# Four graph layers in one kernel: layer 1 aggregates before it multiplies, and the end of layer 3 is ordered anew

## The chip, the cores and the metric

The kernel runs on one core of a Trainium2 chip. The metric is the device time of one execution in microseconds; each time given for a kernel is the median of several runs. Four engines compute: TensorE (PE, matrix products and transposes), VectorE (DVE), ScalarE (ACT) and GpSimd (POOL). SyncE (SP) issues most transfers.

## The reference

The graph has 1024 nodes of 512 features and 16384 edges from `src` to `dst`. Four layers follow each other, each inside `x = layernorm(x + layer(x))`:

```
L0: h = x @ W0 + b0;  adj = row-normalised symmetric 0/1 adjacency with self loops
    relu(dw0*h + dw1*adj@h + dw2*adj@adj@h + dw3*adj@adj@adj@h)
L1: agg = segment_sum(x[src], dst);  agg @ W1.T + b1
L2: x @ wc + segment_sum((x @ wn)[dst], src) / counts + bias
L3: per head h of 8:  Wx = x @ Ws[h] + Wb[h]   (64 columns)
    s = leaky_relu(Wx[dst].a1 + Wx[src].a2 + ab);  alpha = softmax of s over the edges of a dst
    out_h = segment_sum(alpha * Wx[src], dst)
```

In layer 1 the sum over edges is linear. With C the matrix of edge counts, C (x W1^T) = (C x) W1^T, so the product by the weights may stand on either side of the gather.

## The kernel before, in words

**Tiles.** Nodes lie in 8 tiles of 128. `xcur` holds x, `cst` the counts C (source in partitions, target in columns) in f16, `cts` its transpose, `adj` the adjacency. The eight PSUM banks `ps[:, 0..7]` hold 512 f32 columns each. For precision an f32 value is held as two f16 numbers, high and low: a product by weights is three matmuls for each of four blocks of 128 features (hi*hi, hi*lo, lo*hi; `three`, L723), so 12 per tile of 128 nodes and 512 columns; a product by C is two (C is exact).

**Order.** Each engine executes its own queue in the order written, and semaphores join them. No planner is involved: the order is what the text says. Loops over tiles (`Fori`) run two tiles per turn.

**The end of layer 0.** The third hop (`step`, L911) makes one tile of 16 matmuls after another into bank t. `total0` (L1414) takes each from its bank with two VectorE operations and raises `y_ready`. `moments` and `scales` (L1353, L1345) on VectorE and `norm` (L525) on ScalarE make the norm; ScalarE writes the high part into `cur[:, 1, 0]` and the f32 value into `xcur`; GpSimd (L409, L412) then makes the low part (`x_lo`) and adds the next bias (`xb_ready`).

**Layer 1.** TensorE transposes each tile of x (`transposes`, L902: 8 matmuls of 128x128 per tile), ScalarE copies it to `xTs` (`xT_evict`, L536), TensorE multiplies by W1 (`products1`), ScalarE and VectorE take the result z from PSUM as high and low part (`z_hi`, `z_lo`), and `gather` (L953) multiplies by C: 16 matmuls of 512 columns per tile. The transposes of tiles 0 and 1 stand ahead of the third hop's last tile; those for layer 2 ahead of the gather's last tile. `total1` (L1444) adds the result to x, and the norm follows as before. Layer 2 has two products per tile (wc and wn) and another gather.

**Layer 3's beginning.** Per tile TensorE makes x @ W3 and the score columns, ScalarE two exponentials (`exps`, L546), VectorE `wx_evict` (L1466) and `y_whole` (L1474, an operation of 128x1024 f32 from two SBUF inputs), ScalarE the high part of y (`y_upper`), and VectorE the low part (`y_lower`, L1479, two SBUF inputs too). For tiles 5 and 6 GpSimd makes the low part (L417). `exps` of tile t waits for the low part of tile t-2, whose buffer `yf` it reuses. Behind the last y, VectorE computes a bound of the scores (`lim`, L1505 to L1509), TensorE transposes it (L1057), and VectorE turns it into the flag (L1512, L1513) on which all engines branch (`mode`). TensorE meanwhile multiplies y by C (`dense_part`, L1026), four early units tile by tile, the other twelve after the branch. The scores u go through memory (`u_rows`, SP, L331 and L335) and come back as rows for the masks.

**Heads.** For each of 8 heads VectorE makes 8 masks (L1525 or, from a row that ScalarE prepared at L645, L1529), TensorE 8 tiles of 16 matmuls (`head_tile`, L1086). `combine_open` (two VectorE operations from PSUM, L1543 and L1546) and `combine_close` (three, L1552 to L1557) turn a head's sums into output; GpSimd adds it to `xcur` (L424). The tables `OPEN_AT` and `CLOSE_AT` say after which mask each stands.

**Tail.** Heads 6 and 7 are done together in three groups of tiles (`LAST_BANKS`: 0-2, 3-5, 6-7). ScalarE scales their sums (`scaled_sum`, L624), `last_sum` (L1565) does the rest on VectorE, with the norm's statistics over the last 128 columns; `stats` (L1559) takes those of the other columns, `last_moments`, `last_scales` and the norms (`NORM_ACT` on ScalarE, L668, `NORM_DVE` on VectorE, L1597) end a group, and SP sends each tile out, in order of tiles (L341).

Of the kernel before, what the change touches and what calls it, by code (L numbers as in the profile page):

```python
# [26 lines left out]
P = 128  # L27
N = 1024
D = 512
# [27 lines left out]
ASCALE = 1.0 / 32  # L57
# [22 lines left out]
OPEN_AT = {31: 0, 38: 1, 43: 2, 49: 3, 55: 4, 63: 5}  # L80
# [3 lines left out]
STAT_COLS = (0, 5 * DH, PAIR * DH, D)  # L84
NORM_ACT, NORM_DVE = (0, 1, 3, 4, 6), (2, 5, 7)
# [10 lines left out]
def build(nc, x, xT, src, dst, W0, b0, dw, W1T, b1, wc, wn, b2, W3, W3T, b3, b3T, aw, ab, out):  # L96
    with ExitStack() as ctx:
# [248 lines left out]
        def _(pool):  # L346
# [92 lines left out]
        def _(act):  # L439
# [85 lines left out]
            def norm(layer, t, i):  # L525
# [6 lines left out]
                if layer < 3:  # L532
                    act.activation(cur[:, 1, 0, t, :], xcur[:, t, :], ACT.Identity, bias=b, scale=r).then_inc(S["x_hi"], 1)  # L533
                act.activation(xcur[:, t, :], xcur[:, t, :], ACT.Identity, bias=b, scale=r).then_inc(S["x_ready"], 1)  # L534

            def xT_evict(layer, t, i):  # L536
                act.wait_ge(S["xT_done"], t + (layer * NT + 1))
# [3 lines left out]
            def z_hi(layer, t, i):  # L541

                act.wait_ge(S["z_done"], t + (layer * NT + 1))
                copy(cur[:, 0, 0, t, :], ps[:, 4 + i, :], 1 / WSCALE).then_inc(S["z_hi"], 1)

            def exps(t, i):  # L546
                act.wait_ge(S["uvc_done"], t + 1)
                if isinstance(t, int) and t == NT - 1:
                    act.wait_ge(S["y_lo_pool"], 1)
                else:  # L550
                    act.wait_ge(S["y_lo"], t + 1)
# [10 lines left out]
            for layer in range(3):  # L562
# [5 lines left out]
                if layer == 0:  # L568
                    act.wait_ge(S["w_lo"], 4)
                    act.wait_ge(S["cnt_row"], 1)  # L570
# [3 lines left out]
                if layer < 2:  # L574
                    xT_evict(layer, 2, 0)
                    z_hi(layer, 0, 0)
# [20 lines left out]
                else:  # L597
                    with act.Fori(0, NT // 2 - 2) as r:
                        for i in (1, 0):
                            t = r * 2 + (2 - i)  # L600
                            z_hi(layer, t, i)
                            xT_evict(layer, t + 2, i)
                    xT_evict(layer, NT - 1, 1)
                    z_hi(layer, NT - 3, 1)
                    z_hi(layer, NT - 2, 0)
                    z_hi(layer, NT - 1, 1)
# [10 lines left out]
            with act.If(flag(act, 2)):  # L617
                act.activation(std[:, 0:1], epsc[:], ACT.Sqrt).then_inc(S["warm"], 1)

                def sum_of(h, t):  # L620
                    return ps[:, 2 + 2 * (t // 3) + h - PAIR, t % 3 * YW:t % 3 * YW + DH + 1]
# [42 lines left out]
                def last_norms(b):  # L664
                    act.wait_ge(S["scale8"], b + 1)
                    for t in range(*LAST_BANKS[b]):
                        if t in NORM_ACT:
                            act.activation(xcur[:, t, :], xcur[:, t, :], ACT.Identity, bias=nmr[:, t:t + 1],  # L668
                                           scale=rstd[:, t:t + 1]).then_inc(S["out_act"], 1)

                act.wait_ge(S["warm"], 3)
                for b in range(2):
# [4 lines left out]
                last_norms(0)  # L677
                scaled_sums(PAIR + 1, 2)
                deviations(1)
                last_norms(1)  # L680
                deviations(2)
                last_norms(2)
            with act.Else():
                act.wait_ge(S["y_lo"], NT)
                act.wait_ge(S["y_lo_pool"], 2)
# [34 lines left out]
        def _(pe):  # L720
# [206 lines left out]
            transposes(0, 0, 0)  # L927
            transposes(0, 1, 1)
            step(NT - 1, False)

            def per_tile(layer, products, before_last=None):
# [9 lines left out]
                pe.wait_ge(S["xT_in2"], layer * NT + NT - 2)  # L941
# [6 lines left out]
            def product(layer, name, bank, done, free, n, t):  # L948
                pe.wait_ge(S["xT_in2"], t + (layer * NT + 1))
# [3 lines left out]
            def gather(layer, c16, left, done):  # L953

                pe.wait_ge(S["xT_in2"], (layer + 1) * NT)
                pe.wait_ge(S["y_ready"], (layer + 1) * NT)

                def tile(t, parts, first=False):
                    for c in parts:
                        for j in range(NT):  # L960
                            if first:
                                pe.wait_ge(S["z_lo"], layer * NT + j + 3)
                            for v in range(2):
                                ins = mm(ps[:, t, :], c[:, j, bass.ds(t * P, P)], cur[:, 0, v, j, :],  # L964
                                         start=c is c16 and j == 0 and v == 0,
                                         stop=c is parts[-1] and j == NT - 1 and v == 1)
                    ins.then_inc(S[done], 1)

                def tiles(parts):
# [4 lines left out]
                    transposes(layer + 1, 0, 0)  # L974
                    transposes(layer + 1, 1, 1)
                    tile(NT - 1, parts)

                pe.wait_ge(S["big_in"], 1)
                with pe.If(flag(pe, 1)):
                    if layer == 0:  # L980
                        pe.wait_ge(S["left_in"], NT)
                        with pe.Fori(0, NT) as t:
                            pe.wait_ge(S["left_t"], t + 1)
                            for j in range(NT):
                                ins = pe.transpose(bank16(7)[:, j * P:(j + 1) * P], c_left[:, j, bass.ds(t * P, P)], id16[:])
                            ins.then_inc(S["left_done"], 1)
                        pe.wait_ge(S["left_t"], NT + 1)
                    tiles((c16, left))
                with pe.Else():
                    tiles((c16,))  # L990
# [776 lines left out]
```

## Time and profile before

| | us |
|---|---|
| median of 3 runs (415.71 to 415.84) | 415.73 |
| the profiled execution's own time | 415.07 |
| its span, first to last instruction | 413.3 |
| TensorE busy | 381.1 (92%) |
| VectorE busy | 281.0 (68%) |
| ScalarE busy | 249.1 (60%) |
| GpSimd busy | 97.4 (24%) |
| mean granted TensorE clock, share of full | 0.992 |

A line of the timeline gives the start within the span, the length, engine, line of the kernel, what is written and read, and in brackets the idle time before it and what ended that. Matmul lengths overlap their neighbours, so TensorE's pace is read from the distance of two starts. Operations of one kind in a row are merged; their count stands behind the x.

### The profile page before, as it was taken

How to read it: one execution, taken by the hardware profiler on the slowest of the kernel's cores; microseconds unless marked ns; L12 is line 12 of the kernel's file. 1: busy time of each engine (PE TensorE's matmuls, PEld its weight loads, DVE VectorE, ACT ScalarE, POOL GpSimd, SP SyncE). 2: the span in 40 equal slices, each digit the busy share in tenths (PEclk: the TensorE clock that was granted, in tenths of full speed). 3: DMA queues.
4: the chain of work that ended last, by engine and by line, in shares of the span. 5: the costliest groups of instructions: out<-in, count | busy, mean ns of one | idle time of the engine just before them, and what ended most of it. 6: DMA issues, size and time to landing. Idle time of an engine off the chain costs nothing. (4 is left out here: it accounts for less than half of the span.)

```text
span 413.3 us, 8534 instructions
## 1 busy us (share of the span) xinstructions
PE 381.1 (92%) x2908; PEld 227.0 (55%) x2908; DVE 281.0 (68%) x604; ACT 249.1 (60%) x404; POOL 97.4 (24%) x87
## 2 busy tenths in 40 slices
PE   1799888999999999899999999999897999999990
PEld 1344436544444454444445444445555889999990
DVE  7678999729994774225533222554698588999995
ACT  9789777485712356613545221257674899999433
POOL 4520000049900275302644000133104000021110
PEclk9999999999999999999999999999999999999996
DMA  5940005005000000000000000000000313130005
GB/s 193 389 145 2 1 1 205 2 0 205 0 0 2 0 0 2 0 2 1 2 0 2 0 0 2 0 2 0 2 0 8 100 51 103 54 100 7 2 3 207
DMA packets 10040, 18.53 MB, mean 45 GB/s; under 512 B 2128, under 2 KB 2320, under 8 KB 10000
## 3 DMA queue, kind: packets, MB, share of 16 engines
q1 hardware_dynamic: 9136, 14.86, 10.4%
q10 hardware_dynamic: 864, 3.15, 2.4%
q8 instruction: 24, 0.39, 0.4%
q14 instruction: 16, 0.13, 0.1%
HBM read 15.87 MB, written 2.13 MB: 44 GB/s over the span
## 5 line engine op out<-in xcount | busy, mean ns | idle before, releaser
L732 PE MATMUL ps<-big,xTs 128*128 128x512 f16 x384 | 86.2, 379 | 2.9 <-ACT xTs L441 2.9
L732 PEld LDWEIGHTS ps<-big,xTs 128*128 128x128 f16 (+1 forms) x384 | 36.6, 98 | 44.6 <-issue 3.1
L645 ACT ACTIVATE big<-big,uvt 128x1024 bf16<-128x1024 f32 x55 | 58.9, 1149 | 0.0
L409 POOL TENSOR_TENSOR big<-xcur,big x24 | 27.7, 1156 | 128.4 <-ACT xcur L534 128.4
L533 ACT ACTIVATE big<-xcur,nmr,rstd (+1 forms) x24 | 19.5, 813 | 37.8 <-DVE nmr L1351 37.8
L441 ACT ACTIVATE big<-ps 128x512 f16<-128x512 f32 (+2 forms) x25 | 14.5, 579 | 42.1 <-PE ps L732 32.7
L765 PE MATMUL ps<-big,xTs 128*128 128x512 f32 x64 | 34.7, 638 | 0.0
L1361 DVE SCALAR_TENSOR_TENSOR big<-ps,big 128x512 f32 (+1 forms) x16 | 11.0, 690 | 31.0 <-ACT big L441 31.0
L383 POOL TENSOR_TENSOR big<-xTs,big 128x2048 f16<-128x2048 f32 x4 | 16.3, 4097 | 58.8 <-ACT big L441 58.8
L1029 PE MATMUL ps<-big,cst 128*128 128x260 f16 x256 | 29.9, 275 | 0.0
L786 PE MATMUL ps<-adj,cts 128*128 128x80 f16 (+31 forms) x128 | 21.1, 268 | 8.9 <-DVE c L1245 4.7
L1245 DVE TENSOR_TENSOR c<-c,ps 128x80 f32 (+31 forms) x64 | 23.1, 362 | 9.1 <-PE ps L786 5.9
L786 PEld LDWEIGHTS ps<-adj,cts 128*128 128x128 f16 x128 | 11.2, 107 | 31.3 <-issue 15.9
L916 PE MATMUL ps<-big,adj 128*128 128x512 f16 x128 | 28.1, 379 | 0.0
L441 ACT ACTIVATE xTs<-ps 128x1024 f16<-128x1024 f16 (+1 forms) x24 | 23.9, 1017 | 6.9 <-PE ps L908 6.9
L964 PE MATMUL ps<-big,cts 128*128 128x512 f16 x128 | 28.0, 379 | 0.0
L964 PE MATMUL ps<-big,cst 128*128 128x512 f16 x128 | 28.0, 379 | 0.0
L898 PE MATMUL ps<-big,adj 128*128 128x512 f16 x128 | 27.8, 379 | 0.0
L1029 PEld LDWEIGHTS ps<-big,cst 128*128 128x128 f16 x256 | 24.2, 96 | 4.7
L464 ACT ACTIVATE cts<-iota_lo,early 128x128 f16<-128x128 f16 x80 | 25.4, 391 | 0.4
L424 POOL TENSOR_TENSOR xcur<-xcur,c 128x512 f32<-128x512 f32 x6 | 7.1, 1183 | 69.4 <-DVE c L1557 69.4
L1226 DVE TENSOR_TENSOR adj<-adj,early 128x160 f16<-128x160 f16 (+31 forms) x64 | 22.3, 388 | 0.1
(205 smaller groups left out, 689.3 us busy)
## 6 DMA issues: line engine op xcount, KB each, us to landing
big<-u_rows ACTq DMA_DIRECT2D x6, 512.0 KB, 3.6
xTs<-in_xT SPq DMA_DIRECT2D x2, 1024.0 KB, 9.2
xcur<-in_x SPq DMA_DIRECT2D x1, 2048.0 KB, 17.6
out<-xcur SPq DMA_DIRECT2D x8, 256.0 KB, 2.2
big<-in_W SPq DMA_DIRECT2D x1, 1024.0 KB, 5.9
cts<-in_W3T SPq DMA_DIRECT2D x1, 1024.0 KB, 13.1
xTs<-in_W1T SPq DMA_DIRECT2D x1, 1024.0 KB, 5.3
xTs<-in_wc SPq DMA_DIRECT2D x1, 1024.0 KB, 8.2
```

Source lines behind the costliest of these rows:

```text
L409: pool.tensor_tensor(cur[:, 1, 1, t, :], xcur[:, t, :], cur[:, 1, 0, t, :], ALU.subtract).then_inc(S["x_lo"], 1)
L441: return act.activation(o, i, ACT.Copy, scale=scale, **kw)
L464: act.activation(square[:, i % 2, c, :], iota_lo[:], ACT.Square, bias=chunks(nslo[:], mine[i])[:, c:c + 1]).then_inc(S["lo_square"], 1)
L645: act.activation(above[:, a % AHEAD, :], uf[:, h % 2], ACT.Relu, scale=BIG, bias=vb[:, j, h:h + 1]).then_inc(S["above_in"], 1)
L732: return mm(bank, lhs(k)[a], rhs(k)[b], start=start and k == 0 and n == 0, stop=stop and k == KT - 1 and n == 2)
L765: ins = mm(bank, xT32[:, k, t * P:(t + 1) * P], w0raw[:, k, :], start=k == 0, stop=k == KT - 1)
L786: ins = mm(ps[:, WINDOW_BANKS[w % 4], 0:n], left, hot_key[:, r, w % 2 * NC * n:(w % 2 + 1) * NC * n].rearrange("p (k c) -> p k c", c=NC)[: ...
L898: ins = mm(ps[:, t, :], adj[:, j, t * P:(t + 1) * P], cur[:, 1, v, j, :], start=n == 0 and v == 0, stop=n == NT - 1 and v == 1)
L916: ins = mm(ps[:, t, :], adj[:, j, bass.ds(t * P, P)], cur[:, 0, v, j, :], start=n == 0 and v == 0, stop=n == NT - 1 and v == 1)
L964: ins = mm(ps[:, t, :], c[:, j, bass.ds(t * P, P)], cur[:, 0, v, j, :], start=c is c16 and j == 0 and v == 0, stop=c is parts[-1] and j == ...
L1029: ins = mm(ps[:, DENSE_BANK[i], 0:4 * (DH + 1)], cst[:, j, t * P:(t + 1) * P], yh[:, j, v, 4 * half:4 * half + 4, DH + 1:YW], start=j == 0 ...
L1245: tt(cells, cells, ps[:, WINDOW_BANKS[w % 4], 0:NT * m].rearrange("p (a w) -> p a w", w=m), ALU.add).then_inc(S["win_free"], 1)
```

## The change

Layer 1 first multiplies x by the counts, with x as the stationary and C as the moving operand, which gives the aggregate already transposed in eight banks (four blocks of features times two halves of the nodes). ScalarE and VectorE take them into `xTs` as high and low part (`agg_hi`, `agg_lo`), and the product by W1 writes its tiles into banks 0 to 7. The transposes of x and the evictions of z in layer 1 are gone. In layer 3's beginning, the low parts of y of tiles 5 and 6 are made by VectorE. In the tail, head 5's sums are scaled by ScalarE, `stats(0)` covers 256 columns and stands ahead of head 5's close, `stats(1)` covers 128 and stands behind `last_sum(0)`, and ScalarE makes all norms but that of tile 7. Some semaphore increments that nobody waits for are dropped.

```diff
-ASCALE = 1.0 / 32
+ASCALE = 1.0 / 8
-OPEN_AT = {31: 0, 38: 1, 43: 2, 49: 3, 55: 4, 63: 5}
+OPEN_AT = {31: 0, 38: 1, 43: 2, 49: 3, 55: 4}
-STAT_COLS = (0, 5 * DH, PAIR * DH, D)
-NORM_ACT, NORM_DVE = (0, 1, 3, 4, 6), (2, 5, 7)
+STAT_COLS = (0, 4 * DH, PAIR * DH, D)
+NORM_ACT, NORM_DVE = (0, 1, 2, 3, 4, 5, 6), (7,)
@@ GpSimd
-            for t in (NT - 3, NT - 2):
-                pool.wait_ge(S["y_hi"], t + 1)
-                pool.tensor_tensor(yh[:, t, 1], yf[:, t % 2].rearrange("p h e d -> p h (e d)"), yh[:, t, 0],
-                                   ALU.subtract).then_inc(S["y_lo_pool"], 1)
@@ ScalarE
+            def agg_hi(a):
+                act.wait_ge(S["agg_done"], a + 1)
+                half, k = a // KT, a % KT
+                copy(xTs[:, 0, k, half * HALF:(half + 1) * HALF], ps[:, a, :], ASCALE).then_inc(S["agg_hi"], 1)
-            for layer in range(3):
+            with act.Fori(0, NT // 2) as r:
+                for i in range(2):
+                    norm(0, r * 2 + i, i)
+            act.wait_ge(S["w_lo"], 4)
+            for a in range(NT):
+                agg_hi(a)
+            for layer in range(1, 3):
...
+                h = PAIR - 1
+                act.wait_ge(S["head_done"], h + 1)
+                act.wait_ge(S["x_added"], h - 1)
+                for t in range(NT):
+                    scaled_sum(h, t)
                 for b in range(2):
                     scaled_sums(PAIR, b)
                     scaled_sums(PAIR + 1, b)
                 deviations(0)
                 scaled_sums(PAIR, 2)
-                last_norms(0)
+                last_norm(0)
+                last_norm(1)
                 scaled_sums(PAIR + 1, 2)
+                last_norm(2)
                 deviations(1)
-                last_norms(1)
+                last_norm(3)
+                last_norm(4)
                 deviations(2)
-                last_norms(2)
+                last_norm(5)
+                last_norm(6)
@@ TensorE
             pe.wait_ge(S["big_in"], 1)
-            transposes(0, 0, 0)
-            transposes(0, 1, 1)
             step(NT - 1, False)
+            def aggregate(parts):
+                for half in range(2):
+                    for j in range(NT):
+                        pe.wait_ge(S["x_lo"], j + 1)
+                        for k in range(KT):
+                            for c in parts:
+                                for v in range(2):
+                                    ins = mm(ps[:, half * KT + k, :], cur[:, 1, v, j, k * P:(k + 1) * P],
+                                             c[:, j, half * HALF:(half + 1) * HALF],
+                                             start=c is cst and j == 0 and v == 0,
+                                             stop=c is parts[-1] and j == NT - 1 and v == 1)
+                            if j == NT - 1:
+                                ins.then_inc(S["agg_done"], 1)
+            pe.wait_ge(S["y_ready"], KT)
+            with pe.If(flag(pe, 1)):
...
+            with pe.Else():
+                pe.wait_ge(S["y_ready"], NT)
+                aggregate((cst,))
+            def product1(t):
+                three(ps[:, t, :], cols(xTs, t), weight("W1")).then_inc(S["linear1_done"], 1)
+            pe.wait_ge(S["agg_lo"], KT)
+            for t in range(KT):
+                product1(t)
+            pe.wait_ge(S["agg_lo"], NT)
+            for t in range(KT, NT - 1):
+                product1(t)
+            transposes(1, 0, 0)
+            transposes(1, 1, 1)
+            product1(NT - 1)
...
-            def products1(t, i):
-                product(0, "W1", 4 + i, "z_done", "z_lo", t + 1, t)
-            per_tile(0, products1)
-            products1(NT - 1, 1)
-            gather(0, cst, c_left, "gather1_done")
@@ VectorE
-            norm_loop(0, total0, products_in1)
-            products_in1(1, 1)
-            with dve.Fori(1, NT // 2) as r:
-                for i in range(2):
-                    products_in1(r * 2 + i, i)
+            norm_loop(0, total0)
...
+            def agg_lo(a):
+                half, k = a // KT, a % KT
+                nodes = slice(half * HALF, (half + 1) * HALF)
+                dve.wait_ge(S["agg_hi"], a + 1)
+                stt(xTs[:, 1, k, nodes], ps[:, a, :], ASCALE, xTs[:, 0, k, nodes], ALU.mult, ALU.subtract).then_inc(S["agg_lo"], 1)
+            for a in range(NT):
+                agg_lo(a)
             def total1(t):
-                dve.wait_ge(S["gather1_done"], t + 1)
+                dve.wait_ge(S["linear1_done"], t + 1)
                 dve.wait_ge(S["xb_ready"], t + 1)
-                tt(xcur[:, t, :], ps[:, t, :], xcur[:, t, :], ALU.add).then_inc(S["y_ready"], 1)
+                stt(xcur[:, t, :], ps[:, t, :], 1 / (WSCALE * ASCALE), xcur[:, t, :], ALU.mult, ALU.add).then_inc(S["y_ready"], 1)
...
             y_whole(NT - 2, 0)
+            y_lower(NT - 3, 1)
             wx_evict(NT - 1, 1)
...
             stt(lim[:, 3:4], lim[:, 1:2], VMAX * BIG, lim[:, 3:4], ALU.is_le, ALU.mult).then_inc(S["lim_in"], 1)
+            y_lower(NT - 2, 0)
             y_lower(NT - 1, 1)
...
+                def combine_scaled(h):
+                    c = comb[:, h % 2].rearrange("p (a b) d -> p a b d", a=3)
+                    dve.wait_ge(S["head_done"], h + 1)
+                    dve.wait_ge(S["scaled"], NT)
+                    tt(c, c, sums(h)[:, :, :, DH + 1:YW], ALU.subtract).then_inc(S["comb_ready"], 2)
...
-                combine_close(H - 3)
                 stats(0)
+                combine_scaled(PAIR - 1)
+                combine_close(PAIR - 1)
+                last_sum(0)
                 stats(1)
-                last_sum(0)
                 last_moments(0)
                 last_sum(1)
                 last_moments(1)
-                dve.wait_ge(S["scale8"], 1)
-                last_norm(2)
                 last_sum(2)
                 last_moments(2)
-                dve.wait_ge(S["scale8"], 2)
-                last_norm(5)
                 last_scales(2)
                 dve.wait_ge(S["scale8"], 3)
                 last_norm(7)
```

`scaled_sum` and `sums` take head 5's banks in the new version; `c_left` and `ct_left` serve only the branch for counts above 2048, which isn't taken here.

## Rows read from the trace of the kernel before

**Rows 1.** The page's head: span; busy time and share of each engine, with instructions.

```profile
span 413.3 us, 8534 instructions
PE 381.1 (92%) x2908; PEld 227.0 (55%) x2908; DVE 281.0 (68%) x604; ACT 249.1 (60%) x404; POOL 97.4 (24%) x87
```

**Rows 2.** Busy by window: length, then each engine's busy us, clock, DMA share, GB/s.

```profile
156.79:181.75 24.96, 23.73 (x146) 12.07 (x145) 7.82 (x15) 14.36 (x21) 7.12 (x7) 1.00 0.00 1
181.75:210.27 28.52, 28.52 (x146) 13.42 (x145) 13.93 (x34) 12.17 (x21) 11.92 (x10) 1.00 0.00 1
```

**Rows 3.** TensorE's timeline: start, length, line, operation, count, idle time before and its releaser.

```profile
152.45 1.06 PE L908 MATMUL ps<-id,big 128*128 128x128 f16 x16
...
153.34 3.62 PE L916 MATMUL ps<-big,adj 128*128 128x512 f16 x16
156.79 2.75 PE L732 MATMUL ps<-big,xTs 128*128 128x512 f16 x12
159.38 0.61 PE L908 MATMUL ps<-id,big 128*128 128x128 f16 x8
...
167.45 2.76 PE L732 MATMUL ps<-big,xTs 128*128 128x512 f16 x12 [1.23 <-ACT xTs L441]
```

**Rows 4.** Timeline of VectorE, then GpSimd, around the third hop's tiles 3 and 7.

```profile
142.62 0.75 DVE L1416 SCALAR_TENSOR_TENSOR acc<-ps,winv,acc  x1 [0.44 <-PE ps L916]
...
157.78 0.69 DVE L1419 SCALAR_TENSOR_TENSOR xcur<-acc,xcur 128x512 f32<-128x512 f32 x1
...
151.10 1.16 POOL L409 TENSOR_TENSOR big<-xcur,big  x1 [0.96 <-ACT xcur L534]
```

**Rows 5.** Timeline of VectorE, then ScalarE, in layer 1's norms before.

```profile
188.99 0.69 DVE L1447 TENSOR_TENSOR xcur<-ps,xcur  x1 [1.84 <-PE ps L964]
...
191.07 0.21 DVE L1351 TENSOR_SCALAR nmr<-mv,rstd 128x1 f32 x1
...
206.57 1.94 ACT L441 ACTIVATE xTs<-ps 128x1024 f16<-128x1024 f16 x2
```

**Rows 6.** Timeline, layer 3's beginning: VectorE, GpSimd, TensorE, ScalarE.

```profile
308.53 1.22 DVE L1476 TENSOR_TENSOR acc<-cts,acc 128x1024 f32<-128x1024 f32 x1
309.66 1.24 DVE L1481 TENSOR_TENSOR big<-acc,big 128x1040 f16<-128x1040 f32 x1
...
311.61 2.55 DVE L1476 TENSOR_TENSOR acc<-cts,acc 128x1024 f32<-128x1024 f32 x1
...
315.77 2.81 DVE L1476 TENSOR_TENSOR acc<-cts,acc 128x1024 f32<-128x1024 f32 x1
...
321.18 0.14 DVE L1513 CAST flags<-lim 1x1 int32<-1x1 f32 x1
...
310.93 2.15 POOL L417 TENSOR_TENSOR big<-acc,big 128x1040 f16<-128x1040 f32 x1 [20.53 <-ACT big L441]
315.34 2.16 POOL L417 TENSOR_TENSOR big<-acc,big 128x1040 f16<-128x1040 f32 x1 [2.26 <-ACT big L441]
...
316.00 0.27 PE L1054 MATMUL ps<-id,uvt 128*64 128x128 f32 x1 [1.54 <-DVE uvt L1472]
...
319.22 0.27 PE L1057 MATMUL ps<-id,lim 128*1 128x128 f32 x1 [1.11 <-DVE lim L1509]
...
322.18 1.28 ACT L618 ACT_TABLE_LOAD   x1 [2.35 <-DVE flags L1513]
```

**Rows 7.** Timeline of the tail: VectorE, TensorE, ScalarE.

```profile
383.11 4.89 DVE L1529 TENSOR_TENSOR cts<-big,cst 128x1024 f16<-128x1024 bf16 x8
...
392.68 4.25 DVE L1563 BATCH_NORM_STATS2 early<-xcur 128x6 f32<-128x320 f32 x16
...
400.59 0.56 DVE L1572 TENSOR_TENSOR c<-c,ps 128x390 f32<-128x390 f32 x1
...
394.12 2.88 PE L1091 MATMUL ps<-big,xTs 128*128 128x130 f16 x48
...
408.99 0.81 ACT L668 ACTIVATE xcur<-xcur,nmr,rstd 128x512 f32<-128x512 f32 x1 [0.43 <-DVE nmr L1594]
```

More of the change, by code:

```diff
@@ L547, in exps @@
                 act.wait_ge(S["uvc_done"], t + 1)
[L548 to L551, printed above, removed]
+                act.wait_ge(S["y_lo"], t + 1)
                 for e, f in enumerate((1.0, SLOPE)):
@@ L575, in _ @@
                     xT_evict(layer, 2, 0)
-                    z_hi(layer, 0, 0)
+                    z_hi(0, 0)
                 norm(layer, NT - 2, 0)
@@ L620, in sum_of @@
                 def sum_of(h, t):
+                    if h < PAIR:
+                        return ps[:, 2 + 3 * (h % 2) + t // 3, t % 3 * YW:t % 3 * YW + DH + 1]
                     return ps[:, 2 + 2 * (t // 3) + h - PAIR, t % 3 * YW:t % 3 * YW + DH + 1]
@@ L940, in per_tile @@
                 transposes(layer, NT - 2, 0)
-                pe.wait_ge(S["xT_in2"], layer * NT + NT - 2)
+                pe.wait_ge(S["xT_in2"], (layer - 1) * NT + NT - 2)
                 transposes(layer, NT - 1, 1)
@@ L948, in product @@
             def product(layer, name, bank, done, free, n, t):
-                pe.wait_ge(S["xT_in2"], t + (layer * NT + 1))
+                pe.wait_ge(S["xT_in2"], t + ((layer - 1) * NT + 1))
                 pe.wait_ge(S[free], n)
                 three(ps[:, bank, :], cols(xTs, t), weight(name)).then_inc(S[done], 1)
-            def gather(layer, c16, left, done):
-                pe.wait_ge(S["xT_in2"], (layer + 1) * NT)
-                pe.wait_ge(S["y_ready"], (layer + 1) * NT)
+            def aggregate(parts):
[11 more added lines that the diff above has]
+                                ins.then_inc(S["agg_done"], 1)
@@ new lines, in _ @@
+            pe.wait_ge(S["y_ready"], KT)
+            with pe.If(flag(pe, 1)):
+                pe.wait_ge(S["left_in"], NT)
+                with pe.Fori(0, NT) as t:
+                    pe.wait_ge(S["left_t"], t + 1)
+                    for j in range(NT):
+                        ins = pe.transpose(bank16(7)[:, j * P:(j + 1) * P], c_left[:, j, bass.ds(t * P, P)], id16[:])
+                    ins.then_inc(S["left_done"], 1)
+                pe.wait_ge(S["left_t"], NT + 1)
+                aggregate((cst, c_left))
@@ L958, in tile, with gather2 @@
+            product1(NT - 1)
+            def gather2():
+                pe.wait_ge(S["xT_in2"], NT)
+                pe.wait_ge(S["y_ready"], 2 * NT)
                 def tile(t, parts, first=False):
@@ L961, in tile @@
                             if first:
-                                pe.wait_ge(S["z_lo"], layer * NT + j + 3)
+                                pe.wait_ge(S["z_lo"], j + 3)
                             for v in range(2):
                                 ins = mm(ps[:, t, :], c[:, j, bass.ds(t * P, P)], cur[:, 0, v, j, :],
-                                         start=c is c16 and j == 0 and v == 0,
+                                         start=c is cts and j == 0 and v == 0,
                                          stop=c is parts[-1] and j == NT - 1 and v == 1)
-                    ins.then_inc(S[done], 1)
+                    ins.then_inc(S["gather2_done"], 1)
                 def tiles(parts):
@@ L972, in tiles @@
                         tile(t, parts)
-                    transposes(layer + 1, 0, 0)
-                    transposes(layer + 1, 1, 1)
+                    transposes(2, 0, 0)
+                    transposes(2, 1, 1)
                     tile(NT - 1, parts)
-                pe.wait_ge(S["big_in"], 1)
                 with pe.If(flag(pe, 1)):
[L980 to L988, printed above, removed]
-                with pe.Else():
-                    tiles((c16,))
-            def products1(t, i):
-                product(0, "W1", 4 + i, "z_done", "z_lo", t + 1, t)
-            per_tile(0, products1)
-            products1(NT - 1, 1)
-            gather(0, cst, c_left, "gather1_done")
+                    tiles((cts, ct_left))
+                with pe.Else():
+                    tiles((cts,))
             def products2(t, i):
                 product(1, "wc", 2 + i, "alpha_done", "alpha_in", t + 1, t)
-                product(1, "wn", 4 + i, "z_done", "z_lo", t + (NT + 1), t)
+                product(1, "wn", 4 + i, "z_done", "z_lo", t + 1, t)
             per_tile(1, products2)
@@ L1005, in _ @@
             pe.wait_ge(S["alpha_in"], NT + 2)
-            gather(1, cts, ct_left, "gather2_done")
+            gather2()
             def products3(t, i):
```

67 lines of the change are left out of this document (27 added, 40 removed).

## The prediction

> **What bounds the kernel now.** I read the page's busy line first: TensorE works in 381.1 of 413.3 us, no other engine above 68% [rows 1]. So the end moves mostly by what leaves TensorE's queue or by holes in it. The stretches by window come next: the old layer 1 has two, the products by W1 (24.96 us, TensorE busy 23.73) and the gather (28.52 us, no hole), at full granted clock, 2.4 GHz [rows 2]. TensorE's timeline shows what fills the first: a product of 12 matmuls starts at 156.79, transposes at 159.38, so a product takes 2.59 us, and one product waits 1.23 us for an eviction of ScalarE [rows 3]. The timelines of 308 to 323 us show two holes of TensorE, 1.54 and 1.11 us, both released by VectorE [rows 6]. In the tail TensorE starts its last long group at 394.12, while VectorE's chain runs on to 408.99 [rows 7].
>
> **Layer 1, TensorE.** Removed: the 16 transposes ahead of the third hop's last tile, 153.34 - 152.45 = 0.89 us, and from the product stretch all that is not products: 24.96 - 8 x 2.59 = 4.24 us, which is 48 transposes (0.45 us per tile), the wait of 1.23 and small gaps. Kept: 8 products of 12 matmuls (20.7 us). The gather's 128 matmuls of 512 columns become 128 aggregation matmuls of 512 columns with as many weight loads; their stretch without its 16 transposes is 28.52 - 0.89 = 27.63 us, and I take that unchanged. It has the same alternation of weights, and the third hop runs at that pace too. The 16 transposes for layer 2 stay.
>
> Added: a hole. The transposes used to stand where TensorE now waits for all eight `y_ready`, since the aggregation needs banks 4 to 7 free. After the third hop's end (156.79) VectorE takes its two operations, the second ending at 157.78 + 0.69 = 158.47 [rows 4]; with a semaphore's way 158.6. So the hole is 1.8 us; by its bounds 1.5 (nothing but the two operations) and 5 (if the last tile's whole norm had to be awaited). The norm isn't awaited at once: low parts trail their tile's first operation by 151.10 - 142.62 = 8.5 us plus 1.2 [rows 4], so the last is there 9.7 us after about 156.1, at 165.8. The first half takes a tile per 8 matmuls (1.73 us) from 157.7 on and asks for the last at 169.8: 4 us to spare. The branch on the flag lies beside the hop's last tile (3.45 us). The eight evictions (a ScalarE copy and a VectorE subtraction, as the z evictions of before) lie beside the second half (13.8 us) and, for the last four, beside products 0 to 3 (10.4 us against about 3.5): nothing. They stand in front of the norms of layer 1 on both engines, but these begin only when the first product ends, 2.6 us later.
>
> Net: -0.89 - 4.24 + 1.8 = **-3.3 us**.
>
> **What is late next in layer 1.** Tiles now come each 2.59 us, not 3.45. VectorE needs 191.07 + 0.21 - 188.99 = 2.3 us per tile, and the to and fro with ScalarE about 2.5 [rows 5]: it just keeps up. The transposes for layer 2 are issued after tile 6 and need tiles 0 and 1 alone. ScalarE's norm of tile 4 ends some 7 us after that tile, its first eviction of xT takes 1 us [rows 5], and layer 2's first product asks for it at 8.7 us: 0.7 us to spare. Cost 0, up to 1.5 if VectorE lags 0.3 us per tile. Layer 2 is as before.
>
> **The y_lower calls, from GpSimd to VectorE.** Row first: with GpSimd idle, y_whole takes 1.22 us; beside GpSimd's 310.93 + 2.15 = 313.08 it takes 2.55 and ends 1.08 after GpSimd does; beside the second (ends 317.50) it takes 2.81 and ends again 1.08 after [rows 6]. VectorE stands still until GpSimd is done. Out go 1.33 and 1.59 us of that and the wait of 0.86 for the exponentials, which waited for GpSimd. In come two y_lower of 1.15 us each (pitch of the row at 309.66): one ahead of wx_evict(7), one behind `lim_in`. Step by step on VectorE: y_whole(6) 311.61 to 312.75, y_lower(5) to 313.9, wx_evict(7) to 314.55, exponentials done 314.5, scores 314.75, y_whole(7) to 315.9, `lim_in` 316.55 (was 319.15), y_lower(6) and (7) to 318.8, flag 319.25 (was 321.18 + 0.14 [rows 6]). TensorE: transposes of u at 314.8 in place of 316.00, of lim at 316.75 in place of 319.22 without a hole; y_lower(6) and (7) are there when j = 6 and 7 ask (318.7, 319.6). TensorE reaches the branch 2.5 us earlier; the flag is read by then. ScalarE's table load goes from 322.18 to 320.1, and the rows of u from memory come 1.2 us sooner against an arrival near 323.8: so ScalarE's relayed rows, for which the first masks wait, start some 2.0 us earlier, and 2.2 once ScalarE no longer meets TensorE's dense parts ahead of it (a wait of 0.24 us before). From there VectorE is busy without a gap up to its last masks (383.11 + 4.89 = 388.0 [rows 7]).
>
> The Trainium skill (SBUF — State Buffer, "SBUF: two separate sides") says the pair of ports is an exclusive lock between GpSimd and a VectorE operation with two SBUF inputs, and the one that starts later blocks fully. The rows above agree. By plain sharing, VectorE would keep part of the stretch and the step would bring perhaps half.
>
> **The tail.** VectorE loses combine_open(5)'s scaling (0.8 us) to 8 small ScalarE operations of 0.24 us that lie beside stats(0), and two norms of 0.4 us that go to ScalarE at 0.8. The 16 bn_stats (4.25 us [rows 7]) stay, half of them now behind last_sum(0). With VectorE 2.2 us early: masks end 385.8, close(4) 387.4, stats(0) 390.0, combine_scaled 390.8 (TensorE asks at 394.12 - 2.5 = 391.6), close(5) 392.45, last_sum(0) 392.6 to 396.3. In that GpSimd's addition of head 5 (392.5 to 393.7) overlaps the second operation, which has two SBUF inputs: 0.5 us lost. stats(1) 397.8, last_sum(1) 398.3 (400.59 before [rows 7]), last_sum(2) 402.4, moments done 405.55. ScalarE then has its deviation, norm 5 and norm 6 in a row: 405.9, 406.7, 407.45, against 409.80 before (408.99 + 0.81). Norm 6 stood behind VectorE's scales and now stands behind norm 5; so most of what VectorE saves there is given back. Net for the layer's beginning and tail: **-2.35 us**.
>
> Sum: 415.07 (this profiled execution) - 3.3 - 2.35 = 409.4. The median shown is 0.66 above it: 415.73 - 5.65 = **410.1**.
>
> **Rivals.**
> - *GpSimd isn't what stretches y_whole.* Then VectorE has 2.3 us more with nothing in return, flag and masks come about 1 us later than before, TensorE 0.3. Gain 3.3 - 0.8 = 2.5: 413.2. Against it: the end 1.08 us after GpSimd, twice. 9%.
> - *VectorE and ScalarE don't follow TensorE.* The masks start is set by the rows of u, only 1.2 us earlier, and the tail gives back the rest. Gain 3.3 + 1.0: 411.4. For it: the 0.3 us between the chains even in my sum, and ScalarE's row of three at the end. 19%.
> - *The layer 1 norms lag* behind the 2.59 us pace and layer 2's first product waits up to 1.5 us: 411.6. 9%.
> - *Other side: TensorE's clock falls in the new hole.* It is 1.8 us of idleness where dense work stood, with 128 matmuls of 0.216 us behind it. At 1.2 GHz each costs 0.216 us more; from 26 matmuls on the gain of 5.65 us is gone, and with the whole first half slow the time is 410.1 + 13.8 = 423.9. Against it: the granted clock stays 1.00 through the waits of 1.23 [rows 2, 3]. 4%.
> - The parts fall together without effect (port, lag and hole all at their bad end): within 0.2%. 6%.
>
> The Trainium skill (TensorE: Matmul & The Clock Gate, "The HAM clock gate") has the gate lower the clock of an idle TensorE and release it under work. By that rule the hole is a candidate for the rival above; no row here shows a hole that did lower it ahead of the end.
>
> **How the numbers follow.** Forecast 53%, its own range 409.2 to 411.0 (the hole 1.5 to 2.2, the masks 1.7 to 2.5). The rivals above it reach 413.2, so the range is 408.7 to 413.2. 0.2% (0.83 us) is about what a measurement here tells from nothing. Faster 0.90, within 0.06, slower 0.04.
>
> **What would show it.** After: one hole of about 1.8 us ahead of the aggregation and none within it; products back to back at 2.59 us; from the third hop's end to layer 2's first product 51.0 us (210.27 - 156.79 = 53.5 before; the 16 transposes lay ahead of that stretch). y_whole 1.22 in all eight calls. No hole over 0.4 us in TensorE from 312 us (less 3.3) on. VectorE's second operation of last_sum(0) some 0.5 us longer. I am wrong if y_whole stays at 2.5, if TensorE waits for low parts, or if a stretch at half clock follows the hole.

## The result, and the profile after

The changed kernel takes 411.42 us (median of 4 runs, 411.35 to 411.73) against 415.72 us before (4 runs, 415.41 to 415.84): a ratio of 0.990, 95% interval 0.9888 to 0.9912, or 4.3 us less. The forecast was 410.1 us, 5.65 us less, with a range of 408.7 to 413.2 us.

The head of the page after, to be held against [rows 1]: TensorE has 64 matmuls fewer and is busy 1.7 us less, and the span is 3.8 us shorter.

```profile
span 409.5 us, 8229 instructions
PE 379.4 (93%) x2844; PEld 225.4 (55%) x2844; DVE 278.0 (68%) x603; ACT 244.3 (60%) x406; POOL 92.8 (23%) x85
```

**Layer 1.** TensorE's timeline from the third hop's second tile on (columns as in [rows 3]):

```profile
132.45 24.34 PE L925 MATMUL ps<-big,adj 128*128 128x512 f16 x112
158.35 27.80 PE L968 MATMUL ps<-cst,big 128*128 128x512 f16 x128 [1.57 <-DVE xcur L1451]
185.99 18.29 PE L741 MATMUL ps<-big,xTs 128*128 128x512 f16 x84
204.12 1.06 PE L917 MATMUL ps<-id,big 128*128 128x128 f16 x16
205.02 8.16 PE L741 MATMUL ps<-big,xTs 128*128 128x512 f16 x36
213.01 0.61 PE L917 MATMUL ps<-id,big 128*128 128x128 f16 x8
```

The transposes ahead of the hop's last tile and between the products are gone. The 128 matmuls of the aggregation run from 158.35 to 185.99 in one piece, 27.64 us; the products follow at 18.13 / 7 = 2.59 us each. One hole stands in front, 1.57 us, released by the second operation of `total0`. The windows across it (columns as in [rows 2]) show the granted clock at its higher level, 2.4 GHz, through the hole and behind it:

```profile
156.00:160.00 4.00, 2.43 (x12) 0.97 (x11) 3.10 (x9) 1.82 (x4) 3.00 (x4) 1.00 0.02 4
160.00:186.00 26.00, 26.00 (x123) 11.73 (x121) 3.33 (x7) 6.27 (x12) 5.87 (x5) 1.00 0.00 1
186.00:210.00 24.00, 23.94 (x124) 11.20 (x123) 15.74 (x38) 12.08 (x21) 11.94 (x10) 1.00 0.00 1
```

VectorE and ScalarE in the norms behind the products, the first and the seventh tile, and the first two evictions of layer 2:

```profile
188.78 0.69 DVE L1476 SCALAR_TENSOR_TENSOR xcur<-ps,xcur 128x512 f32<-128x512 f32 x1 [0.77 <-PE ps L741]
...
205.36 0.69 DVE L1476 SCALAR_TENSOR_TENSOR xcur<-ps,xcur  x1
...
206.73 1.91 ACT L437 ACTIVATE xTs<-ps 128x1024 f16<-128x1024 f16 x2
```

VectorE takes (205.36 - 188.78) / 6 = 2.76 us per tile against TensorE's 2.59, so it falls about 1 us behind by the seventh tile.

**Layer 3's beginning.** Timeline, VectorE first, then TensorE and ScalarE, against [rows 6]:

```profile
308.69 1.22 DVE L1505 TENSOR_TENSOR acc<-cts,acc 128x1024 f32<-128x1024 f32 x1
309.83 1.24 DVE L1510 TENSOR_TENSOR big<-acc,big 128x1040 f16<-128x1040 f32 x1
...
311.78 1.22 DVE L1505 TENSOR_TENSOR acc<-cts,acc 128x1024 f32<-128x1024 f32 x1
...
316.11 0.14 DVE L1544 CAST flags<-lim 1x1 int32<-1x1 f32 x1
...
312.01 0.27 PE L1083 MATMUL ps<-id,uvt 128*64 128x128 f32 x1 [0.47 <-DVE uvt L1501]
...
313.96 0.27 PE L1086 MATMUL ps<-id,lim 128*1 128x128 f32 x1
...
317.10 1.28 ACT L619 ACT_TABLE_LOAD   x1 [2.85 <-DVE flags L1544]
```

y_whole takes 1.22 us in these calls too (those of tiles 6 and 7). Of TensorE's two holes, 0.47 us is left of the first and nothing of the second, and TensorE's stretch from the first dense unit (312.45 before, 309.54 after) to the first head (345.16, 339.90) is 30.36 us in place of 32.71.

**The tail.** Timeline of VectorE, then GpSimd, ScalarE and TensorE, against [rows 7]:

```profile
384.25 2.71 DVE L1600 BATCH_NORM_STATS2 early<-xcur 128x6 f32<-128x256 f32 x8
386.87 0.75 DVE L1583 TENSOR_TENSOR c<-c,ps 128x585 f32<-128x585 f32 x1
...
388.62 0.69 DVE L1594 TENSOR_TENSOR c<-c,rdf 128x512 f32<-128x512 f32 x1
391.50 0.56 DVE L1609 TENSOR_TENSOR c<-c,ps 128x390 f32<-128x390 f32 x1 [2.18 <-ACT c L627]
...
396.76 0.50 DVE L1609 TENSOR_TENSOR c<-c,ps 128x390 f32<-128x390 f32 x1
...
389.40 1.18 POOL L420 TENSOR_TENSOR xcur<-xcur,c 128x512 f32<-128x512 f32 x1 [3.81 <-DVE c L1594]
...
390.68 0.72 ACT L627 ACTIVATE c<-ps,qc 128x65 f32<-128x65 f32 x3 [3.60 <-POOL xcur L420]
...
404.11 1.50 ACT L669 ACTIVATE xcur<-xcur,nmr,rstd 128x512 f32<-128x512 f32 x2
...
388.86 2.88 PE L1120 MATMUL ps<-big,xTs 128*128 128x130 f16 x48
```

VectorE closes head 5 at 388.62 + 0.69 and then stands still for 2.18 us; `last_sum(0)` begins at 391.50, though TensorE has been at the next group since 388.86. What holds it is ScalarE's scaling of head 7, and what holds that is GpSimd's addition of head 5. Before, the same two operations stood like this, GpSimd's addition first:

```profile
392.84 1.18 POOL L424 TENSOR_TENSOR xcur<-xcur,c 128x512 f32<-128x512 f32 x1 [2.00 <-DVE c L1557]
...
394.32 0.73 ACT L624 ACTIVATE c<-ps,qc 128x65 f32<-128x65 f32 x3 [1.95 <-PE ps L1091]
```

The addition ended at 394.02, and ScalarE waited for TensorE alone. At the very end SP waits for the last output to land (the line of its own waits: total us, count, longest us):

```profile
SPq L97 <- DMA out<-xcur: 2.7, 1, 2.7
```

Before, the same line read:

```profile
SPq L97 <- DMA out<-xcur: 1.9, 1, 1.9
```

### The profile page after: what moved, and what is told of

Read it like the earlier page. It is cut to its first block, busy times and chain, and to the rows that moved or that the text cites. A ratio compares the mean times of both kernels' runs of the same rounds, so it can differ in the third digit from the quotient of the medians.

```text
span 409.5 us, 8229 instructions
## 1 busy us (share of the span) xinstructions
PE 379.4 (93%) x2844; PEld 225.4 (55%) x2844; DVE 278.0 (68%) x603; ACT 244.3 (60%) x406; POOL 92.8 (23%) x85
## 4 chain that ended last, share of the span: by engine, by line
PE 72%; DVE 16%; issue 5%; ACT 3%; DVEq 2%; POOL 1%; ACTq 0%; POOLq 0%
PE ps L741 15%; PE ps L1120 9%; PE ps L968 7%; PE ps L1013 7%; PE ps L925 7%; PE ps L907 7%; PE ps L1061 7%; PE ps L774 4%; PE ps L897 3%; DVE c L1274 3%; PE ps L886 3%; PE ps L795 2%; DVE big L1510 1%; DVE adj L1255 1%; DVE cts L1560 1%
## 5 line engine op out<-in xcount | busy, mean ns | idle before, releaser
L774 PE MATMUL ps<-big,xTs 128*128 128x512 f32 x64 | 35.7, 655 | 0.0
L437 ACT ACTIVATE xTs<-ps 128x512 f16<-128x512 f32 (+2 forms) x24 | 20.1, 878 | 21.7 <-PE ps L968 19.0
L437 ACT ACTIVATE big<-ps 128x512 f16<-128x512 f32 (+2 forms) x17 | 9.7, 572 | 34.5 <-PE ps L741 24.6
L968 PE MATMUL ps<-cst,big 128*128 128x512 f16 x128 | 27.8, 380 | 1.6 <-DVE xcur L1451 1.6
L968 PEld LDWEIGHTS ps<-cst,big 128*128 128x128 f16 x128 | 12.4, 98 | 16.9 <-DVE xcur L1451 2.1
```

What stands on the lines that cost most here:

```text
L437: return act.activation(o, i, ACT.Copy, scale=scale, **kw)
L774: ins = mm(bank, xT32[:, k, t * P:(t + 1) * P], w0raw[:, k, :], start=k == 0, stop=k == KT - 1)
L968: ins = mm(ps[:, half * KT + k, :], cur[:, 1, v, j, k * P:(k + 1) * P], c[:, j, half * HALF:(half + 1) * HALF], start=c is cst and j == 0 ...
```

## The experiments

Each kernel is timed against runs of the kernel before on the same chip: 415.81 us (415.08 to 415.98, 9 runs) for the first four, 415.6 us (415.11 to 415.88, 9 runs) for the second four.

### The change of layer 1 alone

The kernel before with these functions of the change (bodies left out) and their calls; the low parts of tiles 5 and 6 and the tail stay as before.

```diff
+            def aggregate(parts):
+            def product1(t):
+            def agg_hi(a):
+            def agg_lo(a):
...
```

> The kernel before with the change of layer 1 alone (and the dropped semaphore increments); layer 3's beginning and the tail are those of before. Theory A (the layer 1 term of the prediction is right, -3.3 us; the trace of the changed kernel shows -3.2 between the third hop and layer 2's first products): 415.7 - 3.2 = 412.5 us, and a hole of about 1.6 us ahead of the aggregation. Rival B (the changed kernel reached the third hop 0.7 us later than before, 128.88 in place of 128.16, and that belongs to the new layer 1's code): 413.2 us, and the third hop starts at 128.9 in this trace again. Under A the start of the third hop lies anywhere between 128.1 and 128.9 with no tie to the code.

Measured: 412.02 us (411.94 to 412.07), ratio 0.9913 (0.9899 to 0.9926): -3.8 us. The hole is there (158.19, 1.57 us of waiting). y_whole still takes 2.55 and 2.80 us here.

The third hop starts at 128.71 in this trace, which alone would speak for rival B; but it starts at 128.79 in the trace with only the low parts moved, which has nothing of layer 1, and at 128.15 in the trace with the third buffer, which has all of it. In all twelve traces of this study the start falls on one of two levels, 128.15 to 128.25 (four traces) or 128.71 to 128.90 (eight), and both occur with the old and with the new layer 1. Rival B falls. The two groups part early: two f32 matmuls of layer 0 start at 20.41 to 20.44 in every trace, and the pair takes 1.42 to 1.52 us in the four and 1.67 to 2.02 us in the eight. Here before and changed:

```profile
20.43 1.47 PE L765 MATMUL ps<-big,xTs 128*128 128x512 f32 x2
...
20.42 2.02 PE L774 MATMUL ps<-big,xTs 128*128 128x512 f32 x2
```

By 34 us, at the matmuls of 200 columns, the four are at 33.94 to 34.04 and the eight at 34.49 to 34.58. The level belongs to the execution and not to the kernel: the nine runs of the kernel before beside these experiments are two at 415.08 and seven at 415.73 to 415.98, and each of the four traces at the early level is the fastest run of its kernel, by 0.4 to 0.7 us below the median. What makes the pair slower isn't shown.

The gain is 0.5 us more than the -3.3 of the forecast. From the third hop's start to layer 2's second transposes it is 215.45 - 128.16 = 87.29 us before, 213.01 - 128.88 = 84.13 in the changed kernel and 84.13 here too: -3.2. Another 0.5 us comes in layer 3: from its first product to the first dense unit 312.45 - 284.19 = 28.26 us before, 309.54 - 281.75 = 27.79 changed and 309.36 - 281.58 = 27.78 here. In the traces with the old layer 1, one pause of VectorE stands in its loop that nothing in the profile released; in those with the new one it is missing. Before:

```profile
298.75 1.22 DVE L1476 TENSOR_TENSOR acc<-cts,acc 128x1024 f32<-128x1024 f32 x1 [0.33 <-issue]
```

Why it goes, and whether it makes the 0.5 us, is open.

### The low parts of y alone

```diff
-                pool.tensor_tensor(yh[:, t, 1], yf[:, t % 2].rearrange("p h e d -> p h (e d)"), yh[:, t, 0],
-                                   ALU.subtract).then_inc(S["y_lo_pool"], 1)
...
+            y_lower(NT - 3, 1)
...
+            y_lower(NT - 2, 0)
```

> The kernel before with only the low parts of y of tiles 5 and 6 moved from GpSimd to VectorE. Theory A (GpSimd's two operations made VectorE stand still): y_whole takes 1.22 us in all eight calls, TensorE's holes of 1.54 and 1.11 us shrink to 0.5 and 0, TensorE runs 2.3 us earlier and the end 2.0 to 2.3: 413.5 us. Rival B (VectorE and ScalarE don't follow TensorE, the masks' start is set by the rows of u from memory): the first mask row starts only 1.2 us earlier and the time is 414.6 us. Rival C (y_whole's 2.5 us have another cause): no gain, 415.7 or more.

Measured: 413.35 us (412.84 to 413.52), ratio 0.9942 (0.9929 to 0.9956): -2.5 us. y_whole takes 1.22 us (312.25), and TensorE's timeline has of the two holes

```profile
315.57 0.28 PE L1043 MATMUL ps<-id,uvt 128*64 128x128 f32 x1 [0.47 <-DVE uvt L1461]
```

and none ahead of the transposes of lim. Its stretch from the first dense unit to the first head is 30.38 us in place of 32.71. Theory A holds.

### The new tail alone

The kernel before with the new tail:

```diff
+                for t in range(NT):
+                    scaled_sum(h, t)
...
-                combine_close(H - 3)
                 stats(0)
+                combine_scaled(PAIR - 1)
+                combine_close(PAIR - 1)
+                last_sum(0)
                 stats(1)
-                last_sum(0)
...
-NORM_ACT, NORM_DVE = (0, 1, 3, 4, 6), (2, 5, 7)
+NORM_ACT, NORM_DVE = (0, 1, 2, 3, 4, 5, 6), (7,)
```

> The kernel before with only the new tail (head 5 scaled by ScalarE, stats in the new order, norms on ScalarE). Theory A (ScalarE's scaling of head 7's first tiles waits for GpSimd's addition of head 5, whose buffer it reuses, and the new order has put that addition behind stats(0)): last_sum(0) waits for it, the tail is about 1 us longer than before, 416.6 us. Rival B (the tail as I predicted it, +0.15 us over TensorE's shift, and the missing 1.3 us lie elsewhere): 415.9 us or less.

Measured: 417.25 us (416.63 to 417.45), ratio 1.004 (1.0026 to 1.0054): the tail by itself makes the kernel 1.4 us slower. VectorE's timeline:

```profile
396.82 0.56 DVE L1587 TENSOR_TENSOR c<-c,ps 128x390 f32<-128x390 f32 x1 [2.17 <-ACT c L626]
...
402.07 0.50 DVE L1587 TENSOR_TENSOR c<-c,ps 128x390 f32<-128x390 f32 x1
```

`last_sum(0)` begins at 396.82, as before (396.84), but behind 2.17 us of waiting and with `stats(1)` (1.6 us) still to come; `last_sum(1)` begins at 402.07, before at 400.59 [rows 7].

### The changed kernel with a third buffer

```diff
-        comb = cfree[:, dense_end:dense_end + 2 * OW].rearrange("p (q t d) -> p q t d", q=2, t=OS)
+        comb = cfree[:, dense_end:dense_end + 3 * OW].rearrange("p (q t d) -> p q t d", q=3, t=OS)
...
+def buf(h):
+    return 2 if h == PAIR - 1 else h % 2
...
                     if b == 0:
-                        act.wait_ge(S["x_added"], h - 1)
+                        act.wait_ge(S["x_added"], 5 if h == PAIR else 4)
...
                 act.wait_ge(S["head_done"], h + 1)
-                act.wait_ge(S["x_added"], h - 1)
```

`buf(h)` takes the place of `h % 2` wherever `comb` is used. The last line, a wait ahead of the scaling of head 5, held nothing: in both traces that scaling starts about 0.25 us after TensorE begins head 6.

> The changed kernel with a third buffer for head 5's sums, so that ScalarE's scaling of head 7 reuses a buffer that was added long before. Theory A (that wait is the step missing from my tail): ScalarE's wait of 3.6 us for GpSimd and VectorE's of 2.2 us go, last_sum(0) starts about 1.5 us earlier (at 389.8 to 390.0 in place of 391.5), its second operation is held until GpSimd's addition ends (near 390.6), and the time falls by 1.2 to 1.4 us: 410.1 us. Rival B (VectorE's own work sets the tail and the wait only fills its slack): under 0.4 us, 411.1 us.

Measured: 410.09 us (409.49 to 410.19), ratio 0.9867 (0.9852 to 0.9882): 1.3 us less than the changed kernel. GpSimd, ScalarE and VectorE in its tail:

```profile
388.68 1.18 POOL L424 TENSOR_TENSOR xcur<-xcur,c 128x512 f32<-128x512 f32 x1 [3.81 <-DVE c L1597]
...
388.34 0.73 ACT L631 ACTIVATE c<-ps,qc 128x65 f32<-128x65 f32 x3 [1.99 <-PE ps L1123]
...
389.17 0.56 DVE L1612 TENSOR_TENSOR c<-c,ps 128x390 f32<-128x390 f32 x1 [0.57 <-ACT c L631]
389.77 0.57 DVE L1613 TENSOR_TENSOR c<-c 128x390 f32<-128x390 f32 x1
```

Head 7 is scaled as soon as TensorE has it, VectorE waits 0.57 us in place of 2.18. The second operation of `last_sum(0)` (two SBUF inputs) begins at 389.77, when GpSimd (to 389.86) is just done, and isn't lengthened: the collision that the forecast priced at 0.5 us doesn't occur. From the start of TensorE's last group to the end of the span it is 407.6 - 395.40 = 12.2 us, against 409.5 - 396.12 = 13.4 in the changed kernel and 413.3 - 401.38 = 11.9 before.

### The aggregation starts as soon as its banks are free

```diff
                 for half in range(2):
+                    if half == 1:
+                        pe.wait_ge(S["y_ready"], NT)
                     for j in range(NT):
...
             with pe.Else():
-                pe.wait_ge(S["y_ready"], NT)
                 aggregate((cst,))
```

> The changed kernel, where the aggregation's first half (banks 0 to 3) starts once four tiles are taken from their banks, and only the second half waits for all eight. Theory A (the hole of 1.57 us ahead of the aggregation is on the path, and low parts are there in time: the last ends at 165.2, the first half would ask for it 12.1 us after the third hop's end at 156.65, at 168.7): no hole, 411.4 - 1.6 = 409.8 us. Rival B (the low parts, not the banks, pace the first half): the hole moves into the aggregation as waits for GpSimd, gain under 0.8 us, 410.7 us or more.

Measured: 409.93 us (409.74 to 410.26), ratio 0.9861 (0.9846 to 0.9876): 1.5 us less than the changed kernel. TensorE's timeline:

```profile
157.03 27.80 PE L970 MATMUL ps<-cst,big 128*128 128x512 f16 x128 [0.23 <-issue]
```

There is no wait for GpSimd inside, and 0.23 us ahead of it that nothing released. From the third hop's start to layer 2's second transposes it is 211.68 - 128.90 = 82.78 us, 1.35 less than the 84.13 of the changed kernel: the hole was worth what it lasted.

### Both, and the norm of tile 5 back on VectorE, and the old tail

Third buffer and early start together:

> Third buffer and early start together. If both are on the path one behind the other (theory A of both): 411.4 - 1.3 - 1.6 = 408.5 us. Rival: one hides the other, 409.5 us or more.

Measured: 408.57 us (408.2 to 408.91), ratio 0.983 (0.9816 to 0.9843). They add.

The same with

```diff
-NORM_ACT, NORM_DVE = (0, 1, 2, 3, 4, 5, 6), (7,)
+NORM_ACT, NORM_DVE = (0, 1, 2, 3, 4, 6), (5, 7)
...
                 last_moments(2)
+                dve.wait_ge(S["scale8"], 2)
+                last_norm(5)
                 last_scales(2)
```

> Third buffer and early start, with the norm of tile 5 back on VectorE, in the 0.36 us in which it waits for ScalarE's deviation. Theory A (norm 5 and norm 6 in a row on ScalarE end later than norm 6 alone, and the last three output transfers leave closer together and land later: SP waited 2.7 us for the last landing in the changed kernel and in the old kernel with the new tail, 1.9 us before): 0.4 to 0.7 us less than third buffer and early start without it, 408.0 us. Rival B (norm 5 on VectorE delays its last scales by as much): no difference, 408.5 us.

Measured: 407.85 us (407.57 to 408.16), ratio 0.9812 (0.9799 to 0.9825): 0.7 us less than without the last edit. VectorE, ScalarE, and SP's wait for the last landing:

```profile
401.11 0.48 DVE L1637 TENSOR_SCALAR xcur<-xcur,rstd,nmr 128x512 f32<-128x512 f32 x1
...
401.96 0.81 ACT L673 ACTIVATE xcur<-xcur,nmr,rstd 128x512 f32<-128x512 f32 x1 [0.43 <-DVE nmr L1634]
...
SPq L101 <- DMA out<-xcur: 2.2, 1, 2.2
```

Norm 5 lies in time in which VectorE waited. Norm 6 ends at 401.96 + 0.81 = 402.77, 1.57 us after the moments (done 401.20 in this trace); in the changed kernel the norms of 5 and 6 end at 404.11 + 1.50 = 405.61, 1.74 us after the moments (done 403.87). SP's last wait is 2.2 us in place of 2.7. Together that is the 0.7. How much of the landing belongs to the order of the norms is less sure: the same old tail has a last wait of 1.9 us in two traces (before, low parts alone) and of 2.2 in two others (layer 1 alone and the one that follows).

New layer 1 with the early start and new low parts, but with the tail of before, in its order and with its constants, among them:

```diff
-NORM_ACT, NORM_DVE = (0, 1, 2, 3, 4, 5, 6), (7,)
+NORM_ACT, NORM_DVE = (0, 1, 3, 4, 6), (2, 5, 7)
```

> The change of layer 1 with the early start, the low parts of y on VectorE, and the old tail. Theory A (the terms add up: -3.8 for layer 1, -2.5 for the low parts, -1.6 for the early start, from 415.8): 407.9 to 408.1 us, no worse than the new tail with its third buffer. Rival B (the new tail with the third buffer is worth more than the old one, once its wait is gone): 408.8 us or more.

Measured: 408.09 us (407.7 to 408.54), ratio 0.9821 (0.9808 to 0.9835). The terms add up (3.8 + 1.5 + 2.5 = 7.8 us expected from the parts, 415.6 - 408.09 = 7.5 measured), and the old tail is 0.5 us better than the new one with its third buffer (408.57). Against the 407.85 with norm 5 back on VectorE it is 0.2 us worse, and the runs of the two overlap (407.7 to 408.54, 407.57 to 408.16): no form of the new tail is shown to be better than the old one.

### GpSimd beside y_whole: a read and a write

The changed kernel, with one of these on GpSimd (one execution each), once the high part of tile 5 is there:

```diff
+            pool.wait_ge(S["y_hi"], NT - 2)
+            pool.tensor_tensor(ct_left[:, NT - 1, :], c32[:, NT - 1, :], cst[:, NT - 1, :], ALU.subtract).then_inc(S["junk"], 1)
```

```diff
+            pool.wait_ge(S["y_hi"], NT - 2)
+            pool.memset(acc[:, 5:NT, :], 0.0).then_inc(S["junk"], 1)
```

VectorE waits for `junk` once, behind its last y_lower, when both have long been done.

> The changed kernel with one operation of GpSimd added that nobody uses: once the high part of y of tile 5 is there, it subtracts two rows of tensors that y_whole doesn't touch (128x1024, f32 and f16 read from SBUF, f16 written). Theory A (the two engines exclude each other when both read SBUF twice or by the shared way, whatever the tensors): the call of y_whole that falls beside it takes about 2.5 us in place of 1.22 and ends 1.08 us after GpSimd does. Rival B (the stretch before came from the two engines using the same buffers yf and yh): y_whole stays at 1.22.

GpSimd and VectorE in the trace of the first:

```profile
307.97 2.13 POOL L416 TENSOR_TENSOR acc<-c,cst 128x1024 f16<-128x1024 f32 x1 [20.08 <-ACT big L439]
...
308.66 2.52 DVE L1507 TENSOR_TENSOR acc<-cts,acc 128x1024 f32<-128x1024 f32 x1
```

y_whole's call takes 2.52 us and ends at 311.18, 1.08 us after GpSimd (310.10), though neither touches what the other uses (the name `acc` stands for two separate parts of one allocation). The execution took 412.79 us.

> The same place, but GpSimd only writes: a memset of 128x1536 f32 that nobody uses, of 1.5 to 2.5 us. Theory A (only an operation of GpSimd that reads SBUF holds VectorE's second read; the Trainium skill, SBUF - State Buffer, 'SBUF: two separate sides', says so): y_whole takes 1.22 us beside it. Rival B (any operation of GpSimd holds VectorE): y_whole ends 1.08 us after the memset does.

The same of the second:

```profile
307.89 1.38 POOL L416 MEMSET acc<- 128x1536 f32 x1 [20.03 <-ACT big L439]
...
308.60 1.22 DVE L1507 TENSOR_TENSOR acc<-cts,acc 128x1024 f32<-128x1024 f32 x1
```

y_whole begins while the memset runs (to 309.27) and takes 1.22 us. The execution took 411.42 us. Theory A of both holds: VectorE's operation with two SBUF inputs waits for a GpSimd operation that reads SBUF and not for one that only writes it.

## Why the prediction was right, and where it was not

- *What bounds the kernel.* Right: what was taken from TensorE's queue or holes came back in the time, 3.2 us in layer 1 and 2.35 in layer 3's beginning, and 1.5 more with the hole. The stretches between, layer 2 (68.74 us) and the heads (56.22 us from the first to TensorE's last group), are the same before and after.
- *Layer 1, -3.3 us.* Right in mechanism and size: its own stretch gave 3.16. Transposes and wait went, the hole came at 1.57 us (forecast 1.8, bounds 1.5 to 5), the aggregation ran at the gather's pace (27.64 us against 27.63), and no low part was waited for. From the third hop's end (132.45 + 112 x 0.216 = 156.6) to layer 2's first product (207.8) it is 51.2 us, forecast 51.0. The 3.8 us of this part alone holds 0.5 us more, from layer 3, which no step of mine had.
- *What is late next in layer 1.* Half right. I had VectorE just keep up with a tile each 2.59 us; it took 2.76, and the 0.7 us to spare were used up. ScalarE's first eviction for layer 2 began at 206.73 and took about 1 us, and layer 2's first product started 0.2 us after TensorE was free. The bound of 1.5 us was not reached.
- *The clock in the hole.* The rival fell: granted clock 1.00 (2.4 GHz) in the windows across it.
- *The low parts of y.* Right: 1.22 us for y_whole, TensorE 2.35 us earlier (forecast 2.5), 2.5 us in the time alone. The hole left ahead of the transposes of u is 0.47 us, where I had none over 0.4. The two added operations show that GpSimd's reads were the cause.
- *The tail, +0.15 us.* Wrong, and this is the step that failed. I let `last_sum(0)` begin at 392.6 in the old trace's time, as soon as TensorE and ScalarE had head 7, and did not carry over the wait of `scaled_sums(7, 0)` for GpSimd's sixth addition, which is in the code before as well (`x_added`, h - 1, for the buffer that heads 5 and 7 share). Before, that addition ended ahead of TensorE's head 7 and the wait cost nothing; with `stats(0)` put ahead of head 5's close it comes later than TensorE. My own sum had the addition end at 393.7: with 0.1 us to ScalarE and its 0.7 us of scaling, `last_sum(0)` begins at 394.5, 1.9 us later than I wrote. The collision with that addition, which I priced at 0.5 us, then falls away, and 1.4 us are left, which is what the miss was: from TensorE's last group to the end of the span it is 13.38 us in place of 11.92, +1.46. The new tail alone costs 1.4 us, and a third buffer takes 1.3 of it back (1.2 in that stretch). The small rest is the end: norms 5 and 6 in a row on ScalarE, which I had, and SP's last wait of 2.7 us against 1.9 to 2.2 with the old tail, which I had not.
- *Sum.* In the two traces, stage by stage, it is -3.16 (layer 1), -0.47 (layer 3's products), -2.35 (from the dense units to the heads) and +1.46 (tail), together -4.52 us from the third hop on. Of the 1.13 us that are missing to my -5.65, the tail makes 1.31, layer 1 and the low parts 0.14 and 0.15, and the half microsecond in layer 3 that I did not foresee takes 0.47 back. That the error is no larger is in part luck. In the times, the parts alone are -3.8, -2.5 and +1.4 = -4.9, together measured -4.3. The traces of the parts alone sum to -4.73, so 0.2 of those 0.6 us is there too; the rest is within the intervals of the four ratios (about 0.5 us each way).
- *The rival "VectorE and ScalarE don't follow TensorE"* had the measured time (411.4), but for a reason that did not occur: they followed, and the first masks' start was not set by the rows of u (ScalarE's first relayed row came 5.08 us earlier in the span, 319.57 for 324.65, TensorE's first head 5.26).

## What to carry to other kernels

When a piece of work is put ahead of another on one engine, follow the displaced piece to its last consumer, through the buffers as well: a wait that cost nothing before is in the code and not in the profile. Waits for a free buffer are found in the text (who reuses this index?), and one more buffer may be cheaper than any order. Where a sum of products is linear, the order that yields the transposed result saves transposes and evictions both; let its first half start on the banks that are free. Test the parts of a combined change one by one: here one part cost 1.4 us where the others brought 6.3, and with three small edits more 407.85 us were to be had for 411.42. Test the part against leaving it out, too: repaired by two of those edits, the new tail ends level with the old one (407.85 and 408.09).

## What the runs showed of the hardware

- A VectorE operation with two SBUF inputs that starts beside a GpSimd operation that reads SBUF stands still until that ends: y_whole, 1.22 us alone, ended 1.08 us after GpSimd in both calls before (2.55 and 2.81 us) and beside the added subtraction (2.52 us), with shared tensors or without. Beside a memset of GpSimd it took 1.22 us. The Trainium skill (SBUF — State Buffer, "SBUF: two separate sides") calls the pair of ports that the two engines share an exclusive lock for a whole instruction, taken by a VectorE operation with two SBUF inputs only against a GpSimd operation that reads SBUF. The traces agree.
- Work that no kernel of this study changed ends at one of two levels, by execution: the third hop starts at 128.15 to 128.25 or at 128.71 to 128.90 us, and the two groups part between 20 and 34 us. A term under 1 us is therefore taken from stretches between two events behind that point, not from the spans of two traces.
- A hole of TensorE of 1.57 us in dense work left the granted clock at 1.00.
